# Two-layer transformer block: attention output turned to channel-major by transfers instead of transposes, projections as three rounded products

## What is computed

```
layer 0:  h  = ln(x)*(1+s1)+sh1;  q,k,v = h@qkv_w.T+b;  rope(q), rope(k)
          o  = softmax(q k^T / 4) v            # 16 heads of 16 channels
          x  = x + (o@proj_w.T+b)*g1
          h2 = ln(x)*(1+s2)+sh2;  x = x + (gelu(h2@fc1)@fc2)*g2
layer 1:  the same with rmsnorm, w_qkv, w_ao, a swiglu feed-forward, no gates
          (shifts and scales from a small two-stage conditioning net)
```

## Time and profile before

| what | value |
|---|---|
| median of three runs | 814.73 us |
| the profiled execution, its own time | 818.03 us |
| its span, first to last instruction | 816.1 us |
| busy: PE, DVE, ACT, POOL | 769.3 (94%), 632.6 (78%), 491.0 (60%), 290.6 us (36%) |
| mean granted TensorE clock | 0.962 of 2.4 GHz |
| DMA, mean of 16 engines | 32.7% of the span |

### The profile page before, as it was taken

One profiled execution on the slowest core, in us unless ns is written; L12 is line 12 of the kernel. 1 busy time (PEld: TensorE's weight loads), 2 busy tenths in 40 slices (PEclk: granted clock), 3 DMA queues, 4 the chain that ended last, 5 costly groups with the idle time before them and its releaser, 6 DMA issues.

```text
span 816.1 us, 14249 instructions
## 1 busy us (share of the span) xinstructions
PE 769.3 (94%) x4800; PEld 485.8 (60%) x4800; DVE 632.6 (78%) x1349; ACT 491.0 (60%) x1015; POOL 290.6 (36%) x263
## 2 busy tenths in 40 slices
PE   4999999999999999999999999999999999999496
PEld 3654334466645765566646664668547685776396
DVE  3377898879887897879888999978878879753354
ACT  1114785777657875587758777674666656556132
POOL 0321204534354526334364335332343223222334
PEclk9776999999999999899999999999999999999799
DMA  8475645511234015414322515630254212000000
GB/s 323 130 208 155 191 121 143 155 40 41 84 102 136 14 32 150 135 40 143 79 85 60 144 52 143 183 92 1 65 143 126 57 40 67 2 1 27 1 2 27
DMA packets 34153, 76.27 MB, mean 93 GB/s; under 512 B 4512, under 2 KB 9248, under 8 KB 33824
## 3 DMA queue, kind: packets, MB, share of 16 engines
q1 hardware_dynamic: 34080, 75.35, 32.7%
HBM read 39.42 MB, written 35.65 MB: 92 GB/s over the span
## 4 chain that ended last, share of the span: by engine, by line
PE 72%; DVE 13%; POOL 4%; issue 3%; DMA 3%; ACT 2%; SPq 1%; POOLq 0%; ACTq 0%; DVEq 0%
PE ring L989 17%; PE ps_o L920 11%; PE ps_b L1006 10%; PE ring L893 8%; DVE top L1178 7%; PE ring L906 7%; PE ring L858 7%; PE ring L871 3%; PE ring L959 3%; DMA qt<-top_t 2%; PE ring L931 1%; POOL sines L1531 1%; PE ring L840 1%; POOL hl L1565 1%; PE ring L1020 1%
## 5 line engine op out<-in xcount | busy, mean ns | idle before, releaser
L1178 DVE TENSOR_REDUCE top<-ring 128x1 f32<-128x512 f32 x512 | 321.5, 683 | 42.3 <-PE ring L906 40.7
L1428 ACT ACTIVATE pr<-ring 128x512 f32<-128x512 f32 x512 | 270.2, 605 | 67.0 <-PE ring L893 62.9
L1572 POOL TENSOR_TENSOR act_l<-mlp,act_h 128x256 fp32r<-128x256 f32 x128 | 101.7, 795 | 248.0 <-DVE act_h L1255 248.0
L920 PE MATMUL ps_o<-pr,va 128*17 128x512 f32 x1024 | 133.9, 606 | 0.2 <-ACT pr L1428 0.2
L906 PE MATMUL ring<-kt,qt 48*128 48x512 f32 x512 | 123.3, 459 | 4.5 <-ACT pr L1428 1.3
L893 PE MATMUL ring<-qt,kt 49*128 49x512 f32 x512 | 117.5, 455 | 4.7 <-DMA qt<-top_t 4.2
L1465 ACT ACTIVATE mlp<-ring,col 128x256 f32<-128x256 f32 x128 | 61.1, 477 | 85.5 <-PE ring L989 57.5
L893 PEld LDWEIGHTS ring<-qt,kt 49*128 49x128 f32 x512 | 51.9, 185 | 76.2 <-issue 51.5
L906 PEld LDWEIGHTS ring<-kt,qt 48*128 48x128 f32 x512 | 56.4, 190 | 68.7 <-issue 38.6
L989 PE MATMUL ring<-hh,wl 128*128 128x256 f32 x384 | 83.5, 300 | 6.0 <-issue 3.5
L989 PE MATMUL ring<-hh,wh 128*128 128x256 f32 x384 | 79.4, 289 | 0.0
(11 more groups left out here) (86 smaller groups left out, 1035.0 us busy)
## 6 DMA issues: line engine op xcount, KB each, us to landing
scratch<-high SPq DMA_DIRECT2D x48, 512.0 KB, 5.1
qt<-scratch SPq DMA_DIRECT2D x64, 192.0 KB, 3.5
kt<-scratch SPq DMA_DIRECT2D x64, 192.0 KB, 4.4
scratch<-low SPq DMA_DIRECT2D x16, 512.0 KB, 5.9
mlp<-in_w_split SPq DMA_DIRECT2D x20, 256.0 KB, 3.5
xs<-in_x SPq DMA_DIRECT2D x4, 512.0 KB, 5.1
out_x<-xs SPq DMA_DIRECT2D x4, 512.0 KB, 2.9
pr<-in_w_ada SPq DMA_DIRECT2D x2, 512.0 KB, 6.3
```

The source lines that it names most:

```text
L920: last = nc.tensor.matmul(ps_o[32 * h:32 * h + HD + 1, :], va[:, u % 2, t, QUAD * g + h, :], pr[:, slot, :], start=(t == 0), stop=(t == T ...
L1178: nc.vector.tensor_reduce(top[:, n % 2, c:c + 1], bank[:, :], AX_X, ALU.max, negate=True).then_inc(free, 1)
L1428: nc.scalar.activation(pr[:, at % NP, :], bank[:, :], ACT.Exp, scale=SCALE).then_inc(free, 1)
L1572: nc.gpsimd.tensor_tensor(act_l[:, at % 2, :], src, act_h[:, at % 2, :].bitcast(F32), ALU.subtract).then_inc(act_l_in, 1)
```

## The change

- `output` on PE and DVE, and `o_turn`, are gone. ACT still copies `ps_o` to `ot`. `gather` on SP then issues eight DMAs a quad: four spread each head's row of sums over 16 partitions of `den`, four move each head's 16 rows into `o`, which now is channel-major.
- Twice a unit (for each 128 channels k): DVE `invert` (reciprocal of 128x32), SP `inverse` (to DRAM), SP `spread` (back, each head's row repeated over its 16 partitions, into `late`), POOL `share` (o times late), ACT `channels` (adds the v bias, rounds to `hh`), DVE `rest` (to `hl`).
- `take_v` moves from DVE to ACT, without the bias. `cast` (the rounding to `act_h`) moves from DVE to ACT. `modulated` writes the rounded `hh` and then `hf`; POOL `rest` makes `hl`, now for the attention's norm too. The feed-forward has its own `hh2`, `hl2`.
- `qk`, `v` and `project` become three fp32r products each, two contraction tiles each: six instructions in place of four. Their weights are split into `qh`, `ql`: four chunks at the start through the stage buffers, four more for layer 1 through `late`.
- `high` and `low` are written over `raw` and `sines`, so `take` (ACT) and `sine` (POOL) wait until the spill before has landed.
- The conditioning net's weights come in six chunks through the stage buffers, and the net runs beside quad 0. All ticks are new.

```diff
-    return pieces + [(tick, engine, "output", n) for tick, engine in zip(at["output"], ("act", "pe", "dve"))]
+    return pieces + [(at["output"][0], "act", "output", n), (at["output"][1], "sp", "gather", n)]
...
+def share_pieces(u, k):
+    return [("dve", "invert", u, k), ("sp", "inverse", u, k), ("sp", "spread", u, k), ("pool", "share", u, k),
+            ("act", "channels", u, k), ("dve", "rest", u, "o", k)]
...
+                def gather(n):
+                    u, g = quad_of(n)
+                    k, at = g // 2, g % 2 * STACK
+                    sp.wait_ge(o_free, n + 1)
+                    if u:
+                        sp.wait_ge(hl_in["o"], KC * (u - 1) + k + 1)
+                    for h in range(QUAD):
+                        r = at + HD * h
+                        sp.dma_start(den[r:r + HD, k, :], ot[32 * h + HD:32 * h + HD + 1, :]).then_inc(moved, 16)
+                    for h in range(QUAD):
+                        r = at + HD * h
+                        sp.dma_start(o[r:r + HD, k, :], ot[32 * h:32 * h + HD, :]).then_inc(moved, 16)
...
+                def inverse(u, k):
+                    sp.wait_ge(inv_in, KC * u + k + 1)
+                    sp.dma_start(dens[k].rearrange("(p n) -> p n", p=P), inv[:, k, :]).then_inc(inv_out, 16)
...
+                def spread(u, k):
+                    sp.wait_ge(inv_out, 16 * (KC * u + k + 1))
+                    sp.wait_ge(*side_free("spread", u, k))
+                    sp.dma_start(late[:, :], dens[k].rearrange("(h n) -> h n", n=L).unsqueeze(1).to_broadcast(
+                        [P // HD, HD, L])).then_inc(spread_in, 16)
...
                 def q_and_k(u, c):
...
-                        last = nc.tensor.matmul(bank[:, :], w[:, k, c * P:(c + 1) * P], hf[:, k, :],
-                                                start=(k == 0), stop=(k == KC - 1))
+                    for wp, hp in ((ql, hh), (qh, hh), (qh, hl)):
+                        for k in range(KC):
...
+                            last = nc.tensor.matmul(bank[:, :], wp[:, i, k, at:at + P], hp[:, k, :],
+                                                    start=(n == 0), stop=(n == 3 * KC - 1))
...
                 def take(u, c):
...
-                        ac.wait_ge(cos_in, at)
-                        ac.wait_ge(sin_in, at)
+                        ac.wait_ge(low_in, at)
+                        ac.wait_ge(*spill_landed((at - 1) // 2, (at - 1) % 2))
...
+                    nc.scalar.activation(high_of(name)[:, k, :], bank[:, :], ACT.Identity, bias=bias, scale=scale
+                                         ).then_inc(hh_in[name], 1)
+                    nc.scalar.activation(hf[:, k, :], bank[:, :], ACT.Identity, bias=bias, scale=scale
+                                         ).then_inc(emptied_in, 1)
...
+                def share(u, k):
+                    gp.wait_ge(spread_in, 16 * (KC * u + k + 1))
+                    gp.wait_ge(moved, 16 * 2 * QUAD * (NQ * u + 2 * k + 2))
+                    nc.gpsimd.tensor_tensor(o[:, k, :], o[:, k, :], late[:, :], ALU.mult).then_inc(share_in, 1)
```

More of the change, by code:

```diff
@@ L112, in first_pieces @@
               ("pe", "norm_turn", 0, 0)]
-    pieces += [("act", "modulated", 0, 0, k) for k in range(KC)]
+    for k in range(KC):
+        pieces += [("act", "modulated", 0, 0, k), ("dve", "rest", 0, "h1", k)]
     for pair in range(2):
@@ L123, in first_pieces @@
         pieces += [("dve", "widen", b), ("pe", "gates", b), ("dve", "gates", b)]
[L124 to L133, removed]
- -1302,
[L135 to L152, removed]
- -892,
[L154 to L196, removed]
+    return pieces
+FIRST_AT = (-2107,
+ -1131,
+ -1973,
+ -1793,
+ -1951,
+ -1855,
+ -1943,
+ -1892,
+ -1681,
+ -1377,
+ -1580,
+ -1289,
+ -1423,
+ -1034,
+ -1302,
+ -1200,
+ -1205,
+ -1200,
+ -985,
+ -1582,
+ -943,
+ -1153,
+ -1412,
+ -948,
+ -868,
+ -1144,
+ -1200,
+ -1039,
+ -962,
+ -1039,
+ -764,
+ -699,
+ -678,
+ -753,
+ -675,
+ -430,
+ -533,
+ -618,
+ -1067,
+ -511,
+ -531,
+ -748,
+ -590,
+ -672,
+ -892,
+ -787,
+ -1475,
+ -828,
+ -830,
+ -1475,
+ -828,
+ -765,
+ -1330,
+ -823,
+ -672,
+ -840,
+ -526,
+ -381)
 def top_pieces(n):
@@ new lines @@
+SPLIT_AT = ({'act': (-1644,
+          -1297,
+          -1259,
+          -683,
+          -185,
+          -132,
+          434,
+          -66,
+          -8,
+          -445,
+          139,
+          172,
+          225,
+          230,
+          282,
+          365,
+          405,
+          420,
+          454,
+          468,
+          482,
+          491),
+  'dve': (-1304,
+          -1019,
+          -992,
+          -777,
+          1213,
+          -63,
+          -558,
+          439,
+          -748,
+          88,
+          162,
+          211,
+          238,
+          299,
+          301,
+          387,
+          402,
+          410,
+          490,
+          522,
+          527,
+          527),
+  'load': (-1826,
+           -1631,
+           -1029,
+           -970,
+           -669,
+           -541,
+           -478,
+           -256,
+           -207,
+           -18,
+           7,
+           105,
+           110,
+           229,
+           263,
+           272,
+           289,
+           315,
+           333,
+           446,
+           471,
+           510)},
+ {'act': (36, 39, 53, 82, 83, 91, 139, 155),
+  'dve': (49, 53, 61, 82, 109, 121, 139, 157),
+  'load': (-38, 19, 29, 54, 70, 71, 74, 114)})
@@ L436, in post_pieces @@
     at = POST_AT[POST_KIND[u]]
[L437 to L438 removed]
+    pieces = []
+    for k in range(KC):
+        pieces += [(tick, *piece) for tick, piece in zip(at["o"][k], share_pieces(u, k))]
     pieces += [(at["project"][t], "pe", "project", u, t) for t in range(T)]
@@ L464, in pre_pieces @@
     pieces = norm_pieces(u, 0, at["norm"])
+    pieces += [(at["rest"][k], "pool", "rest", u, "h1", k) for k in range(KC)]
     for c in range(NC):
@@ L821, in store @@
                     sp.dma_start(out_v[j], xs[:, j]).then_inc(x_out, 16)
-                whole_program("sp", {"load": load, "load_w": load_w, "spill": spill, "fill": fill, "top": top_row,
+                whole_program("sp", {"load": load, "load_w": load_w, "late": late_load, "spill": spill, "fill": fill, "gather": gather,
+                                     "inverse": inverse, "spread": spread, "top": top_row,
                                      "store": store})
@@ L1603, in prologue @@
     s_ada = [name(f"ada{i}") for i in range(3)]
-    s_wf = [name(f"wf{i}") for i in range(3)]
     fill = name("fill")
```

913 lines of the change are left out of this document (477 added, 436 removed).

## The result

The changed kernel took 876.84 us, the median of four runs (870.61 to 887.79); the kernel before, on the same chip, 812.81 us. The ratio is 1.075, 95% interval 1.063 to 1.087: slower, where 785 us and a gain were forecast. Ratios leave out executions in a slower state of the chip, here the one of 887.79 us, so by the ratio the change costs 61 us and by the medians 64. The profiled execution's span is 868.7 us, with a mean granted clock of 0.924 (before 816.1 us and 0.962). First the same stretches as in the earlier trace rows: the four of layer 0, the three of layer 1, the tail.

A forecast was written before the change was run, and what follows sets the result against it. PE was taken to bound the seven stretches, until ACT reached its ceiling in layer 0. The terms -17.2-16.8-5.0+9.5 = -29.5 us turned 818.0 into 788.5, less 3.3 to the median: 785 us, range 768 to 817.

The forecast's parts named there:

- so I price this at nothing: SP's queue: a gather blocking until ACT's copy costs 0, the next quad's `top` and fill being queued ahead.
- inside the seven stretches a microsecond off PE is a microsecond off the time: Four stretches of layer 0, three of layer 1: PE's saving shortens the time one for one, until another engine is full.
- my 6.3: PE, per stretch: 6.3 us saved by dropped transposes and fp32r q, k, v and `project`; 4.2 in the last stretch.
- SP's queue takes the place: Rival, chance 0.17: `top` stands behind a blocking gather and PE's scores wait; 831 us, from 815 to 860.
- ACT gives the rest back: Rival, chance 0.18: layer 0 stays at 88 us, exponentials standing behind casts and doubled writes; 807 us, 801 to 816.
- Layer 0: Four stretches of 88.0 us: 4.3 us gained in each, ACT becoming the bound at 83.7 us; -17.2 us.
- Layer 1: Three stretches of 91.0 us: PE's saving counts whole, 6.3+6.3+4.2; -16.8 us.
- Head and first attention: Conditioning net leaves the head, DVE loses work in the first attention; -5 us together, between +4 and -10.
- The tail: ACT's copy to first `project` grows from 4.1 to 13.9 us; +9.5 us net, between +6 and +14.
- my 3.5: Tail, `spread`: 3.5 us, a fill's time, called the weakest term; by the slowest-dimension rule 2 us more, time 787.
- The 512-column product: PE, q and k: full fp32r products over 512 columns 0.24 us apart, taken as twice 0.120; -1.6 us a stretch.
- ACT's load: ACT in layer 0: +11.8 us a stretch, 62.3 to 74.1 us; at the 88.6% ceiling this needs 83.7 us.

The follow-up runs named there:

- the one other order that I tried: Changed kernel with only SP's order altered in quads 4 to 15 (two `top` ahead of gather or fill, one gather ahead of spill): 874.75 us, 1.074.
- without a gather: Changed kernel with the gather's DMAs removed, `den` and `o` holding ones, all else kept, output not the reference's: 830.37 us, 1.020.
- lighter-PE experiments: Kernel before with query and key products over half the contraction: 821.98 us, 1.012; with DVE's reductions at half width too: 806.46 us, 0.993.
- ACT lighter: Changed kernel with no gather, ACT's `cast` cut to 2 columns and `take_v` of units 2 to 7 to one head: 831.74 us, 1.020.
- five issues: Changed kernel with `den`'s four gather DMAs a quad merged into one, five gather issues in place of eight, same result: 839.55 us, 1.031.

## Why the prediction was wrong

**The step that failed first** is the one on SP's queue, "so I price this at nothing", with the ground that `top` and fill of the next quad are queued ahead of the gather. Its size was near: eight issues took 5.0 us where I had 4.4. Its cover was not there. The `top` of some quads and the fill of others stand behind it, and the one other order that I tried did not help: `top`, fill, spill and gather all feed the same PE. The issue records sum to 186 us over the run before and to 377 after; in layer 0 SP issues for 44 to 49 us of each stretch. I read this so: a queue that is idle half of the time is not free if its work comes due in bursts and what waits for it is the head of each quad. That step costs 46 us (876.8 against 830.4; 45 by the ratios). What carries that cost into PE isn't settled wait by wait: the lateness of `top` went from 49 to 5 us in another order, and to 1 us with `top` on ACT, and the time did not fall.

**The second** is what the whole sum rests on: "inside the seven stretches a microsecond off PE is a microsecond off the time". The PE time did come off, if less than forecast: without a gather, start to start over three stretches of layer 0, q, k, v, `project` and the two transposes went from 53.5 to 39.7 us, 4.6 a stretch for my 6.3. None came out at the end:

```profile
122.10:396.10 274.00, 259.37 (x1605) 155.87 (x1603) 214.61 (x411) 214.56 (x474) 126.06 (x109) 0.95 0.35 97
```

These three stretches, without a gather, are 274.0 us long; before, they were 266.8. PE's idle time in them is 14.6 us, 9 more than before. The lighter-PE experiments on the kernel before show the same without anything else of the change. I read PE's few waits as proof that PE sets the time. In a program in strict order on every engine, with the order fitted to these durations, it also means that PE's work fills the gaps: taken out, it leaves gaps.

**What took the gain back.** Idle time, the clock after it, and slower scores. Over the same three stretches without a gather, from start to start: -13.8 us by q, k, v, `project` and the transposes, +9.1 by idle time, +10.8 by scores and peaks (72.3 to 83.2), +1.1 by the rest, in all +7.2. Of the scores and peaks 26 now start at 1.2 GHz, where 4 did; at full clock they come further apart too, every 0.205 us for 0.184, and why isn't known. With PE at 98% the clock in layer 0 was 0.98; at 90% it was 0.92, so PE ran at 1.2 GHz for a sixth of that time. The Trainium skill, TensorE: Matmul & The Clock Gate, section "What's actually happening", says that the throttled state is the default and that activity releases it; the traces agree, since 0.97 became 0.95 by a cut of PE's work alone.

**The rivals.** SP's queue takes the place (0.17, 831 us, to 860) had the mechanism, the place and the sign. I had scores breaking even at 0.9 us a quad of waiting; the waits are 0.97 (31.1/32), and the change was at +64. That threshold charged them against 29.5 us of gain that never came. "ACT gives the rest back" fell: ACT lighter moved nothing.

**Term by term.** All from the profiled executions. Layer 0: forecast -17.2, measured +35, without a gather +7. Layer 1: forecast -16.8, measured +8, without a gather 0. Head and first attention: forecast -5, measured -1, without a gather -5 (the kernel before with one `top` issue had them 8 us shorter as well, so this stretch varies by more than the forecast). Without a gather the tail is 6 us longer than before, and the parts add up to +9; by the ratio it is +16, since the profiled execution before, 818.03 us, was longer than its kernel's median. The tail was right: 74.5 us for 73 to 74, 14.7 us from ACT's copy to `project` for 13.9:

```profile
794.19 0.61 ACT ot L1582
...
799.22 1.98 DMA o<-ot
801.22 0.36 DVE inv L1346
801.61 1.42 DMA dens<-inv
803.04 3.67 DMA late<-dens
...
806.78 1.27 POOL o L1734
808.07 0.73 ACT hh L1591
808.80 0.04 issue
808.85 2.94 PE ring L1133 x12
```

`spread` landed in 3.67 us for my 3.5; the 2 us more that I had worked out from the rule of the Trainium skill, DMA: Bandwidth & Descriptors, section "Why a DMA increments its semaphore by 16 and not by 1", on a slowest dimension of 8 did not come. The 512-column product was right too: 0.233 us apart for 0.24. ACT's load was forecast at 74.1 us a stretch of layer 0 and was 71.4 (285.4/4), DVE's 66.9 and 71.6 (286.6/4); 2 us a stretch of what DVE has too much are `cube`, whose mean rose from 0.437 (L1262) to 0.577 us (L1410) at the same median. Waits of `take` for a landed spill, priced at nothing, were 4.9 us in three times, with no wait of PE behind them in the profile.

**Open.** Which link paces the stretches of the kernel before is not settled. It is not PE's work, alone or with DVE's, and 119 us less of DVE's gave 8 us; ACT's was tried only in the changed kernel. Left are the chains between them (`take`, rope, spill, fill, peaks, `top`, scores) and the order. Nor did I try new ticks fitted to five issues, a way in which PE's 4.6 us a stretch might still come out.

## What to carry to other kernels

Before counting a saving on the busiest engine, ask what it would wait for next; in a strict, fitted order, test it by cutting that engine's work in the old kernel, which costs one run. Price added DMAs by the issue time in their queue, and by what stands behind each at its worst quad, not by the queue's mean idle time; merge transfers that differ by a partition stride first (10 issues a quad to 6 gave back 46 of the 61 us here, by the ratios). And a PE that began to wait was granted less clock here (0.98 to 0.92 in layer 0), so a wait costs more than its own length.

## What was not expected of the hardware

- A DMA holds the issuing engine for 0.58 to 0.66 us on SP (gather: 169 us for 256), 0.65 us on ACT in the pair above and 0.49 us on POOL (61.4 us for the 128 of `o`), whether it moves 2 KB (`den`) or 32 KB (`o`). On SP they land 1.9 (`den`) and 2.0 us (`o`) after the start of the issue, by the median. The Trainium skill, DMA: Bandwidth & Descriptors, section "Issuing engines are not separate DMA queues", calls the sequencer's time to start a DMA usually small relative to the DMA; these rows disagree: it is a third, and eight in a row take 5.0 us.
- One DMA may read or write partitions at a stride (`ot[HD:P:32]`, `qt[SHIFT:P:STACK]`), at the price of one issue: 0.58 us for the merged `top` (with five gather issues) against 1.38 us for the pair in the rows above.
- The moved cast of 128x256 takes 423 ns on ACT (L1634) against 311 on DVE; back on DVE in the changed kernel it took 374 ns there.
